# Expert stage: TensorE reads the experts of a loop body's eight tiles at the head of the body

## The reference, cut to what matters

```python
x = x + gnn(layernorm(x), adj, ...)          # two graph layers over 128 graphs of 128 tokens
xt = layernorm(x).reshape(-1, 384)           # 16384 tokens
route_prob = softmax((xt @ enc_w + enc_b) @ sw_w + sw_b)
routes = argmax(route_prob)                  # one of 8 experts for each token
h = gelu(xt @ w1[expert] + b1[expert])       # 384 -> 64
out = (h @ w2[expert] + b2[expert]) * max(route_prob)     # 64 -> 384
x = x + out
```

## Time and profile before

| what | before |
|---|---|
| time, median of 3 runs | 2208.31 us (2204.04 to 2211.86) |
| profiled execution, from its first to its last instruction | 2205.2 us |
| TensorE's mean granted clock, as a share of full speed | 0.987 |
| busy share of the span: PE, PEld, DVE, ACT, POOL | 95%, 92%, 75%, 67%, 64% |

### The profile page before, as it was taken

How to read it: one execution, slowest core, us unless ns; L and a number is a source line. 1 busy time by engine, 2 the same in 40 slices (tenths; PEclk the granted TensorE clock), 3 DMA queues, 4 the chain that set the end, 5 groups by cost and what they waited for, 6 DMA issues and landing times. The chain is left out here.

```text
span 2205.2 us, 53282 instructions
## 1 busy us (share of the span) xinstructions
PE 2102.8 (95%) x13580; PEld 2035.4 (92%) x13581; DVE 1643.7 (75%) x5452; ACT 1484.5 (67%) x3901; POOL 1413.6 (64%) x3348
## 2 busy tenths in 40 slices
PE   6999999999999999999999999999999999678786
PEld 5999999999999999999999999999999999566665
DVE  5777777777777777777777777777777777667675
ACT  4777776677766767767676676767767677365564
POOL 2556666666666666666666666666666666546666
PEclk9999999999999999999999999999999999889998
DMA  7101111311111111111111111111111111166774
GB/s 190 31 26 49 49 37 49 114 46 46 41 49 47 48 46 44 49 49 49 43 47 49 49 49 42 45 49 46 50 41 46 49 46 37 55 197 203 218 226 132
DMA packets 94221, 153.39 MB, mean 70 GB/s; under 512 B 17621, under 2 KB 70619, under 8 KB 93954
## 3 DMA queue, kind: packets, MB, share of 16 engines
q1 hardware_dynamic: 75844, 99.61, 15.8%
q0 software_dynamic: 17408, 50.62, 6.1%
q10 hardware_dynamic: 704, 0.10, 0.0%
HBM read 96.11 MB, written 57.32 MB: 70 GB/s over the span
## 5 line engine op out<-in xcount | busy, mean ns | idle before, releaser
L416 PE MATMUL bank<-wT_hi,hT_hi 128*128 128x384 f32 x2304 | 795.6, 345 | 5.6 <-ACT bank L616 3.0
L418 PE MATMUL bank<-wT_hi,hT_lo 128*128 128x384 f32 x2304 | 772.8, 335 | 0.0
L417 PE MATMUL bank<-wT_lo,hT_hi 128*128 128x384 f32 x2304 | 771.7, 335 | 0.0
L416 PEld LDWEIGHTS bank<-wT_hi,hT_hi 128*128 128x128 f32 x2304 | 434.1, 188 | 10.8 <-ACT bank L616 9.1
L417 PEld LDWEIGHTS bank<-wT_lo,hT_hi 128*128 128x128 f32 x2304 | 434.1, 188 | 0.0
L418 PEld LDWEIGHTS bank<-wT_hi,hT_lo 128*128 128x128 f32 x2304 | 433.0, 188 | 0.0
L1167 POOL TENSOR_TENSOR hT_lo<-hT,hT_hi 128x384 fp32r<-128x384 f32 x256 | 259.8, 1015 | 22.6 <-ACT hT_hi L681 22.2
L676 ACT ACTIVATE hT<-bank 128x384 f32<-128x384 f32 x256 | 125.9, 492 | 207.8 <-PE bank L408 148.1
L652 ACT CAST right_hi<-bank 128x384 fp32r<-128x384 f32 x256 | 122.5, 479 | 203.1 <-PE bank L418 201.9
L1222 POOL TENSOR_SCALAR_AFFINE_SELECT deltaT_hi<-turned_hi 128x128 fp32r<-128x128 f32 x256 | 81.4, 318 | 245.8 <-ACT turned_hi L658 231.8
L408 PE MATMUL bank<-hT 128*128 128x128 f32 x1536 | 213.3, 275 | 0.0
(11 more groups left out here) (201 smaller groups left out, 5153.2 us busy)
## 6 DMA issues: line engine op xcount, KB each, us to landing
tok<-buckets SPq DMA_DIRECT2D x72, 388.0 KB
x_in<-in_x_dram SPq DMA_DIRECT2D x128, 192.0 KB, 2.6
x_res<-in_x_dram SPq DMA_DIRECT2D x128, 192.0 KB, 2.4
adj_in<-in_adj_dram SPq DMA_DIRECT2D x128, 64.0 KB, 2.7
buckets<-pads SPq DMA_DIRECT2D x9, 388.0 KB
out_dram<-out_rows,row_ids POOLq DMA_INDIRECT x144
buckets<-rows,dest_words POOLq DMA_INDIRECT x128, 2.8
w_top<-in_L_ffn_w_dram SPq DMA_DIRECT2D x2, 768.0 KB
```

Of the source, the lines that this page charges most:

```text
L416: pe.matmul(o, hi, w_hi, start=False, stop=False, skip_group_check=True)
L417: pe.matmul(o, hi, w_lo, start=False, stop=False, skip_group_check=True)
L418: last = pe.matmul(o, lo, w_hi, start=False, stop=(c == C - 1), skip_group_check=True)
```

## The change

TensorE's read of one expert in each `output` is taken out. `tiles` gets a third argument, `lookup`, which TensorE alone gives. It is called ahead of step 0 (for tiles 0 to 3), at the head of every loop body (for the eight tiles whose `output` stands in the body) and ahead of step 72 (for tiles 68 to 71). It reads these tiles' experts into registers, eight in a loop body, and `output` takes its own from there.

```diff
-            def tiles(eng, step):
+            def tiles(eng, step, lookup=None):
+                if lookup:
+                    lookup(0)
                 for i in range(RING):
                     step(i, i)
                 with eng.Fori(1, TILES // RING) as block_of:
+                    if lookup:
+                        lookup(block_of * RING)
                     for k in range(RING):
                         step(block_of * RING + k, k)
+                if lookup:
+                    lookup(TILES)
                 for i in range(TILES, TILES + DEPTH):
                     step(i, i % RING)
...
+                    expert_of = {}
+                    def experts_of_block(first):
+                        for k in range(RING):
+                            j = first - OUTPUT + k
+                            if there(j):
+                                expert_of[j % RING if isinstance(j, int) else (k - OUTPUT) % RING] = pe.value_load(
+                                    tile_expert[0:1, j:j + 1] if isinstance(j, int) else
+                                    tile_expert[0:1, bass.ds(j, 1)], min_val=0, max_val=E - 1)
                     def output(j, k):
-                        e = pe.value_load(tile_expert[0:1, j:j + 1] if isinstance(j, int) else
-                                          tile_expert[0:1, bass.ds(j, 1)], min_val=0, max_val=E - 1)
+                        e = expert_of[k]
                         pe.wait_ge(gelu_top_ready, j + 1)
...
-                    tiles(pe, step)
+                    tiles(pe, step, experts_of_block)
```

## The result

The changed kernel takes 2260.59 us (median of 4 runs, 2260.12 to 2264.86), the kernel before 2207.9 us on the same chip (4 runs, 2204.04 to 2211.86). The ratio is 1.0238, 95% interval 1.0224 to 1.0251: 52.7 us slower, where I had said 2250, with 2226 to 2276 as range.

The account below looks back on a forecast made before the run. It took the loop between `output` and DVE's combine as the bound. A body of 22.9 + 8.8 + 1.65 = 33.4 us against 28.6 gave +38 over eight, the end +3: +41, from 2205.2 to 2246, stated as 2250, range 2226 to 2276.

Parts of the forecast that it names:

- The mechanism: Expert stage: reads in steps were free; eight at each head push PE back, slow its clock, and waits for `out_rows` return.
- Reads in the steps: In the loop's steps: `hidden` covers the 64 reads, so removing them gains nothing, at most 5.0 us of issue waits.
- Reads, 6.0 us a head: Head of each loop body: eight uncovered reads delay `turn`, `hidden` and `output`, the interval going from 2.76 to 8.8 us.
- Clock, 1.65 us a head: Behind the pause at each of eight heads: the idle array's clock falls once, costing 1.65 us, twice that as upper end.
- Seven other intervals, 22.9 us: Rest of each body: after the pause seven tile intervals take 22.9 us, as at the stage's start, against up to 24.7.
- The tail: Ahead of step 72: four reads of 0.7 us each delay tile 68 and POOL's last eight stores, moving the end by +3.
- Hidden: Rival at the heads: the sequencer is so far ahead that work handed over before covers the reads; chance 0.04.
- Partly absorbed: Rival in the bodies: waits return more slowly, seven intervals take 20.5 us, a body 31.0, time about 2230; chance 0.08.
- The other side: Rival, faster: alternation of intervals breaks up, clock holds, seven intervals take 18.6 us, a body 27.4, time 2201; chance 0.04.
- Longer and disturbed: Rival: reads of 0.9 us, slow clock twice as long, no gain from the pause; body 38.0 us, time 2287; chance 0.14.

Follow-up runs that it names:

- e1: The changed kernel with the read of one expert put back into each `output` as well, the reads at the heads staying: 2256.74 us, ratio 1.0249.
- e2: The kernel before with a single read ahead of the stage, whose register all 72 tiles use (output not the reference's): 2199.91 us, ratio 0.9996.
- e5: The changed kernel with each of the eight reads at a head made twice: 2299.21 us, ratio 1.0446.
- e6: The changed kernel with two extra matmuls of unused result ahead of each of the eight reads at a head: 2248.46 us, ratio 1.0212.
- e11: The changed kernel once more, unaltered, timed against the kernel before: 2257.68 us, ratio 1.0257.
- e4: The changed kernel with 14 extra matmuls of unused result handed over ahead of the eight reads at each head: 2268.0 us, ratio 1.0309.
- e8: The changed kernel with two reads ahead of every second step in place of eight at the head: 2214.38 us, ratio 1.0055.
- e3: The changed kernel with four reads at the head of the body and four ahead of its fifth step: 2250.6 us, ratio 1.022.
- e7: The changed kernel with four reads at the head, four ahead of the fifth step, and two extra unused matmuls ahead of each read: 2239.49 us, ratio 1.0179.

## Why the prediction was right, and where its sizes were off

**The mechanism** was right in each step. Reads in the steps were free as far as the times can tell (e1 against the change, e2 at 0.9996 of the kernel before). At the head shown the sequencer is hardly ahead (0.36 us), and over the eight heads the reads add up and almost nothing covers them (pauses of 6.7 us in the mean; 0.70 us for each further read in e5). Seven of the eight pauses are given to issue, so it isn't only semaphores that hold PE up. The clock is low around the end of each pause (0.50 in windows of 6 us there, 0.88 in the mean of the stretch; in e6, without the pauses, 0.99). The waits for `out_rows` are back by the fourth tile of the body shown.

**The size** was short, +41 us for +52.7. The forecast of the body was 33.4 us; the eight took 277.3 us, 34.7 each. By its terms:

- *Reads, 6.0 us a head.* The pauses were 6.7 us in the mean (53.4 / 8), of which 0.2 had been there before. So the term was some 0.5 short. A read took 0.75 in the earlier trace rows and 0.70 in e5. The rest is disturbed loads, such as the 769 ns at the head shown: the 64 loads took 25.7 us together, 6.3 more than at 304 ns each, or 0.8 a head, less the 0.36 us of cover.
- *Clock, 1.65 us a head.* The eight head intervals were 11.2 us in the mean (10.5 to 11.8). Of that 2.76 is bare, 6.5 the added pause, and 1.9 is left for the clock; e6 gives 1.6 to 1.9 by another way. The price I took, 1.65, is from the one interval behind a pause of 2.59 us, in a window whose mean granted clock was 0.66 after 1.00 in the one ahead of it. It was at most 0.3 too low.
- *Seven other intervals, 22.9 us.* They took 23.45, 0.55 more. The first of them was still at the slow clock (3.34 for 2.65 us), but in e6, where it was bare, the seven took about the same, 23.3 (268.9 less eight heads of 10.3, over 8). So what it lost there was mostly given back by a shorter wait later. The 0.55 is in waits, but it isn't a steady effect: in e11, the same kernel, the seven took 22.95, as I had said.
- These three make 1.3 us a body, 10 in all.
- *The tail*, +3, was +5.0 in the profiled pair: from the first matmul of tile 67 to the end 25.2 us (2233.40 to 2258.6) for 20.2. In e11 it is 23.1, so +2.9, which is the term as I had it. In the profile after, all of the 5.0 lies between the first `output` matmuls of tiles 67 and 68 (8.37 us for 3.42; the last row is a window of all engines):

```profile
2235.03 0.45 PE L1465 MATMUL bank<-w_top,gelu_top 128*128 x1 [1.02 <-DVE out_rows L1562]
2238.26 1.51 PE L1430 MATMUL bank<-ident,n_rows 128*128 128x128 f32 x6 [2.62 <-ACT n2T L1506]
2239.00:2243.00 4.00, 4.00 (x13) 3.46 (x12) 1.62 (x5) 1.06 (x2) 2.20 (x3) 0.50 0.01 0
```

A wait for `out_rows` inside tile 67 held PE up for 1.02 us, and the four reads only began behind it (2235.3). Then came their pause, and a clock of 0.50. In e11 that wait is missing.

**The rivals.** *Hidden*, at 0.04 in the chances, needed a sequencer so far ahead of the array at the heads that work handed over before covers the reads. It is out: PE stood for 6.30 us at the head shown and for 6.7 in the mean of the eight. In e4 the sequencer did get ahead: 56 weight loads and matmuls stood in front of the first load, which started with 3.9 us of their 6.28 still to run (2032.6 to 2036.46), about 34 of the 56. All 56 had been handed over by then, so the run doesn't show how far ahead it could get. What counts at the heads of the change is that little has been handed over there: 0.36 us of work at the head shown. *Partly absorbed* is what e8 does and the change doesn't: short pauses fall where PE waited anyway. *The other side* needed seven intervals in 19.8 us. *Longer and disturbed* has some truth in the loads up to 867 ns, in the clock and in the waits: a body took 34.7 us, about a quarter of the way from my 33.4 to its 38.0.

**My own later misses** were of one kind. For e3, e4, e6 and e7 I expected more than came, since I took a remedy (half a pause, added array work) as free of side effects. Two short pauses brought the slow clock twice and left waits for `out_rows` between them, and the added matmuls kept the sequencer itself busy.

## What to carry to other kernels

A read into a register of TensorE's sequencer cost nothing that these runs can tell where matmuls that were handed over before it still ran (e1, e2), and its full 0.7 to 0.8 us where the sequencer had just caught up with its engine, as at the head of this loop's body (0.36 us ahead). Collecting such reads in one place added them up (eight became 6.7 us) and brought the slow clock with it (0.50 behind the head shown), while one in each step vanished in cover, and two ahead of every second step mostly took the place of waits that were there anyway (e8, 0.55% slower). Before a saving is planned, take the thing away altogether: the kernel with no reads in its steps was as fast as the one with 64 to within 0.2%, so there was next to nothing to win.

## What I hadn't expected of the hardware

Handing matmuls over wasn't free for the sequencer. In e4 it took about 2.4 us for 28 weight loads and 28 matmuls, 43 ns each. In e6, with 64 of them spread between the reads, the heads were only 1.0 us longer than the bare 2.76 and the change's 6.5 of added pause, some 16 ns each. What makes the difference was not tried.

The length of a pause alone didn't say whether the clock fell. In e3 the slow clock came behind 15 of the 16 pauses (2.38 to 3.87 us), but not behind one of 3.03 us that ended at 2198.1. In e8 it came behind 3 of the 32 pauses of 0.7 to 1.6 us. One of the three ended at 2102.85. Here are windows of PE alone behind the pause in e3 and across the end of the one in e8:

```profile
2199.00:2207.00 8.00, 6.08 (x34) 1.00 0.39 128
2102.00:2106.00 4.00, 3.15 (x11) 0.60 0.89 239
```

So in the change a pause of some 6 us (6.7 in the mean) brought it at every head, and in e8 those under 1.7 us seldom did (3 of 32).

The load of one word took about 300 ns mostly (median 304 before, 308 in the change), but up to 867 ns in the bodies. 8 of the 64 took over 400 ns before the change, 21 in the change and 2 in e8. What disturbs them was not tried.

Also, the wait for `out_rows` that bounds this stage in every version has an odd start. In the kernel before, the timeline of all engines at a long step has:

```profile
2032.87 0.34 PE L1450 MATMUL bank<-w_bottom,gelu_bottom 128*128 x1
...
2033.70 1.46 PE L1436 MATMUL bank<-n2T,w_pick 128*128 128x256 f32 x6
...
2036.01 1.14 DVE L1546 SCALAR_TENSOR_TENSOR out_rows<-bank,tok 128x384 f32<-128x384 f32 x2 [0.93 <-remote]
2036.20 0.59 ACT L1490 COPY n2T<-bank 128x512 f32<-128x512 f32 x1 [0.81 <-remote]
```

The last `output` matmul of the tile ended at 2033.21, but DVE's combine began at 2036.01, 0.85 us behind the end of the whole `hidden` (2035.16), after idle time whose releaser the view doesn't name. The semaphore events in the trace do: the earlier store from that buffer (`stored`) had ended at 2026.45, while `y_done` was raised at 2035.99, 2.8 us behind the end that the profile gives the matmul. ACT's copy of the turned tile has the same shape, with PE's signal at 2036.17 for a `turn` that ended at 2033.87. So both wait for PE's signals, and no store is in the way. Why these come so late is open. The ends of matmuls in the profile are modelled, none of these experiments touched it, and most of the 40 us of waiting in the stage hang on it.
